# Graph network with masked attention: one q tile of each head turned by VectorE and DMAs instead of TensorE, and one weight set held

## The reference, cut to what matters

```python
h = jnp.maximum(_layernorm(x, axis=-1), 0.0)
q, k, v = (h @ W + b for each), split in 8 heads of 32
scores = einsum('bqhd,bkhd->bhqk', q, k) * 32 ** -0.5
scores = masked by adj            # -inf in layer 2, -1e9 in layer 3
attn = softmax(scores)            # 1024 x 1024 for each head and batch
out = einsum('bhqk,bkhd->bqhd', attn, v) @ Wo + bo
x = x + out                       # layer 2: + out + layernorm(out)
```

## Time and profile before

| | |
|---|---|
| median of 3 runs | 2798.15 us (2797.14 to 2798.94) |
| the profiled execution | 2797.58 us |
| its span | 2795.7 us |
| TensorE busy | 2762.8 us (99%) |
| VectorE busy | 2250.6 us (81%) |
| ScalarE busy | 2062.7 us (74%) |
| GpSimd busy | 1126.7 us (40%) |
| granted TensorE clock | 0.997 of full speed |
| moved by DMA | 251.32 MB |

### The profile page before, as it was taken

One profiled execution on the slowest core, in us unless ns is written; L12 is line 12 of the kernel. 1 busy time (PEld: TensorE's weight loads), 2 busy tenths in 40 slices (PEclk: granted clock), 3 DMA queues, 4 the chain that ended last, 5 costly groups with the idle time before them and its releaser, 6 DMA issues.

```text
span 2795.7 us, 60283 instructions
## 1 busy us (share of the span) xinstructions
PE 2762.8 (99%) x23520; PEld 2219.0 (79%) x23520; DVE 2250.6 (81%) x4144; ACT 2062.7 (74%) x3711; POOL 1126.7 (40%) x1088
## 2 busy tenths in 40 slices
PE   9999999999999999999999999999999999999998
PEld 7888888687778787878787877787778777778776
DVE  6776766888888888888888888888888888888876
ACT  3000001988888889898889888888888888888886
POOL 2222321225556464637373747242424242415131
PEclk9999999999999999999999999999999999999999
DMA  3001002434343434343434363434344343434333
GB/s 132 31 31 61 31 31 61 103 75 111 78 108 90 108 87 104 88 111 83 116 80 111 87 163 94 103 82 110 83 100 99 90 103 87 110 81 114 85 92 84
DMA packets 170601, 251.32 MB, mean 90 GB/s; under 512 B 33328, under 2 KB 135216, under 8 KB 170320
## 3 DMA queue, kind: packets, MB, share of 16 engines
q1 hardware_dynamic: 169120, 243.14, 34.7%
q0 software_dynamic: 1200, 4.33, 0.5%
HBM read 70.65 MB, written 25.69 MB: 34 GB/s over the span
## 4 chain that ended last, share of the span: by engine, by line
PE 70%; POOL 5%; issue 2%; ACT 2%; DVE 2%; DMA 1%; SPq 0%; POOLq 0%; ACTq 0%; DVEq 0%
PE t_ring_ps L885 28%; PE t_ot_ps L913 15%; PE t_s_ps L872 14%; PE t_ring_ps L855 4%; PE t_ring_ps L856 4%; PE t_ring_ps L857 4%; POOL t_xe L1397 2%; ACT t_T L1074 1%; PE t_ring_ps L945 1%; ACT PT L1080 1%; POOL t_oT_lo L1472 1%; POOL t_ot L1461 1%; DVE t_T L1164 1%; DMA t_R_ot<-inverse_row_sums 1%; DMA inverse_row_sums<-t_rT 1%
## 5 line engine op out<-in xcount | busy, mean ns | idle before, releaser
L1164 DVE CUSTOM_DVE_ANT_0 t_T<-t_s_ps,mask 128x1024 f32<-128x1024 f32 x1024 | 1233.4, 1215 | 114.4 <-PE t_s_ps L872 107.7
L1074 ACT ACTIVATE t_T<-t_T,t_low 128x1024 f32<-128x1024 f32 x1024 | 1170.8, 1150 | 23.5 <-DVE t_low L1164 20.2
L885 PEld LDWEIGHTS t_ring_ps<-ident,t_T 128*128 128x128 f32 x8192 | 933.7, 141 | 213.3 <-issue 72.2
L885 PE MATMUL t_ring_ps<-ident,t_T 128*128 128x128 f32 x8192 | 1088.8, 274 | 7.7 <-ACT t_T L1074 2.8
L1080 ACT ACTIVATE PT<-t_ring_ps 128x512 f32<-128x512 f32 x1376 | 757.3, 597 | 230.0 <-PE t_ring_ps L885 220.5
L872 PE MATMUL t_s_ps<-t_k,t_q 128*128 128x512 f32 x2048 | 727.4, 436 | 1.6 <-DVE t_low L1164 1.5
L1249 DVE COPY PT<-t_ring_ps 128x512 f32<-128x512 f32 x672 | 460.9, 690 | 191.0 <-PE t_ring_ps L885 185.0
L913 PE MATMUL t_ot_ps<-PT,shared 128*32 128x256 f32 x8192 | 494.9, 382 | 0.2 <-ACT PT L1080 0.2
L913 PEld LDWEIGHTS t_ot_ps<-PT,shared 128*32 128x32 f32 x8192 | 240.0, 109 | 217.0 <-ACT PT L1080 45.0
L273 ACT ACTIVATE g_yT_hi<-g_ps 128x512 fp32r<-128x512 f32 x64 | 38.3, 599 | 379.3 <-PE g_ps L205 379.3
L872 PEld LDWEIGHTS t_s_ps<-t_k,t_q 128*128 128x128 f32 x2048 | 309.2, 191 | 5.6 <-DVE t_low L1164 5.0
(11 more groups left out here) (186 smaller groups left out, 3743.3 us busy)
## 6 DMA issues: line engine op xcount, KB each, us to landing
t_q<-t_st_hi SPq DMA_DIRECT2D x256, 128.0 KB, 2.3
t_q<-t_st_lo SPq DMA_DIRECT2D x256, 128.0 KB, 2.4
t_k<-t_st_hi SPq DMA_DIRECT2D x256, 128.0 KB, 2.4
t_k<-t_st_lo SPq DMA_DIRECT2D x256, 128.0 KB, 2.4
t_R_ot<-inverse_row_sums SPq DMA_DIRECT2D x256, 64.0 KB, 2.0
t_oT_raw<-t_ot SPq DMA_DIRECT2D x512, 32.0 KB, 1.9
shared<-x_after_graph_layers SPq DMA_DIRECT2D x8, 1024.0 KB, 6.3
t_xe<-x_after_graph_layers SPq DMA_DIRECT2D x32, 256.0 KB, 3.2
```

The costliest lines, as they stand in the source:

```text
L885: last = nc.tensor.transpose(banks[b][:, i * P:(i + 1) * P], T[u % RING][:, kt * P:(kt + 1) * P], ident[:])
L1074: nc.scalar.activation(T[u % RING][:], T[u % RING][:], ACT.Exp, bias=low[:, u % RING:u % RING + 1], scale=-1.0, accum_out=rsum[:, u:u + 1] ...
L1164: nc.vector.tensor_tensor_reduce(out=T[u % RING][:], in0=s_ps[u % 2][:], in1=mask[:, qt, :], scale=1.0, scalar=3.4e38, op0=ALU.add, op1=AL ...
```

## The change

In each head the q tile 0 (units 0, 8, 16, ... of the job, `FLIPS`) is no longer transposed by TensorE and not copied from PSUM. Once its exponential is done, VectorE transposes its 32x32 blocks into `turned_T` (`turn_T`, one instruction of 128x1024). SyncE writes that tile to DRAM (`move_turned`, one DMA of 512 KB in rows of 512 bytes) and, when it is there, reads it back into `PT` in four DMAs of 128 KB, one for each 32 partitions (`place_turned`). `values` of the next head waits for them. In this way the queries of a tile lie in four chunks of 32 in `PT`; tile 1, which shares its matmuls with tile 0, is copied in the same layout (`from_bank`), and the matmuls over the two tiles read 32 columns at a time.

Of the weights one set is held. Layer 3's are split in job 0 through three small tiles `w_new`, saved in DRAM, and loaded over layer 2's: q, k and v columns in job 7, the output's in job 8.

With it other things move: `values` stands ahead of the block of the group's first unit; the copy of the finished head pair (`copy_ot`) stands at the head of ScalarE's group; the row sums' DMA is split in a write and a later read; `regroup` 0 and the loads of `xe` come at other places of SyncE's order; GpSimd's order changes; tables `EARLY`, `MID`, `NEXT`, `BOTH_ON_ACT` (22 units before, 28 now, none of them a q tile 0) and `RAW_ON_DVE` have new numbers. An output block goes from unit 27 to 19.

```diff
-EARLY = [(1, ("norm", 3)), (11, ("out", 0)), (14, ("out", 1)), (27, ("out", 2)), (30, ("out", 3))]
...
+EARLY = [(1, ("norm", 3)), (11, ("out", 0)), (15, ("out", 1)), (19, ("out", 2)), (26, ("out", 3))]
...
+BOTH_ON_ACT = {2, 6, 10, 11, 13, 14, 15, 17, 18, 19, 22, 25, 26, 27, 30, 33, 34, 39, 41, 42, 43, 46, 50, 53, 54, 59, 62, 63}
+RAW_ON_DVE = {20, 34, 37, 49, 52}
+FLIPS = (0,)
...
-                if key[0] == "T" or key[2] in table:
+                if key[2] in table if key[0] == "B" else key[2] % 8 not in FLIPS:
...
-        w_hi = [as_weights(split[0]), sb("w_hi1", [P, DC, 4 * D], F32R)]
-        w_lo = [as_weights(split[1]), sb("w_lo1", [P, DC, 4 * D], F32R)]
+        w_hi, w_lo = as_weights(split[0]), as_weights(split[1])
+        w_new = [sb(f"w_new{i}", [P, 2, DC, D], F32R) for i in range(3)]
...
+        turned_T = [sb(f"turned_T{i}", [P, N]) for i in range(len(FLIPS))]
...
+        def in_chunks(qt):
+
+            return qt in FLIPS or qt ^ 1 in FLIPS
+
         def pt_of(u, half):
 
             qt, keys = u % NT, slice(half * HT, (half + 1) * HT)
-            return PT[:, qt, keys, :] if u // NT % 2 == 0 else PT[:, keys, qt, :]
+            tiles = PT[:, qt, keys, :] if u // NT % 2 == 0 else PT[:, keys, qt, :]
+            return tiles.rearrange("p g (k q) -> p k g q", k=HT) if in_chunks(qt) else tiles
+
+        def from_bank(ps, u):
+
+            return ps[:].rearrange("p (k g q) -> p k g q", k=HT, g=4) if in_chunks(u % NT) else                 ps[:].rearrange("p (k q) -> p k q", k=HT)
...
-            def spread_rows(job, pr, key):
+            def move_turned(job, h, i):
+
+                n = HEADS * job + h
+                sp.wait_ge(T_turned[i], n + 1)
+                if n:
+
+                    sp.wait_ge(turned_in[i], 64 * n)
+                sp.dma_start(turned_rows[i].rearrange("c p f -> p c f"),
+                             turned_T[i][:].rearrange("p (c f) -> p c f", c=NT)).then_inc(turned_out[i], 16)
+
+            def place_turned(job, h, i):
+
+                n, qt = HEADS * job + h, FLIPS[i]
+                sp.wait_ge(turned_out[i], 16 * (n + 1))
+                if n:
+
+                    sp.wait_ge(av_done, NT * (n - 1) + (HT if qt < HT else NT))
+                for j in range(4):
+                    rows = slice(j * HD, (j + 1) * HD)
+                    sp.dma_start(PT[rows, qt, :, :] if h % 2 == 0 else PT[rows, :, qt, :],
+                                 turned_rows[i][2 * j:2 * j + 2].rearrange("h (g k) f -> k (h g) f", g=4)).then_inc(turned_in[i], 16)
...
+            def save_weights(i):
+
+                sp.wait_ge(w_split, i + 1)
+                for part in range(2):
+                    sp.dma_start(w_scratch[part][:, :, i * D:(i + 1) * D],
+                                 w_new[i % len(w_new)][:, part].bitcast(F32)).then_inc(w_saved[i % len(w_new)], 16)
+
+            def load_weights(cols):
+
+                for i in range(len(w_new)):
+                    sp.wait_ge(w_saved[i], 32 * len(range(i, 4, len(w_new))))
+                for part, to in enumerate((w_hi, w_lo)):
+                    sp.dma_start(to[:, :, cols].bitcast(F32), w_scratch[part][:, :, cols]).then_inc(w_late, 16)
...
+                move_head(job, 0)
                 if before is not None:
-                    for p in range(XE):
-                        load_xe(job - 1, before, p)
-                    spread_rows(job - 1, 3, key_of(job, ("norm", 3)))
+                    write_rows(job - 1, 3, key_of(job, ("norm", 3)))
+                place_head(job, 0)
+                if before is not None:
+                    read_rows(job - 1, 3)
                     regroup(job - 1, 3, (0,))
                 load_head(job, 2, UNITS * job + 8, None)
                 if before is not None:
                     regroup(job - 1, 3, (1,))
+                move_head(job, 1)
                 if after is not None:
 
                     sp.wait_ge(v_moved, job + 1)
@@ -795,32 +861,60 @@
                     sp.dma_start(xa[:], x_of(after, job + 1 - B * after).rearrange("(t p) d -> p t d", p=P)).then_inc(xa_in, 16)
                 if before is not None:
                     regroup(job - 1, 3, (2, 3))
+                place_head(job, 1)
                 load_head(job, 3, UNITS * job + 16, None)
-                spread_rows(job, 0, key_of(job, ("norm", 0)))
+                if job == 0:
+                    save_weights(0)
+                    save_weights(1)
+                move_head(job, 2)
+                write_rows(job, 0, key_of(job, ("norm", 0)))
+                place_head(job, 2)
+                read_rows(job, 0)
                 if before is not None:
                     store(job - 1, before, 0, key_of(job, ("out", 0)))
                     after_store(job - 1, 0)
                     load_xe(job - 1, before, 3)
+                if job == 0:
+                    save_weights(2)
+                    save_weights(3)
                 load_head(job, 4, UNITS * job + 24, (job, 1))
+                if layer != after and after is not None:
+                    load_weights(slice(0, 3 * D))
+                move_head(job, 3)
+                place_head(job, 3)
...
+                move_head(job, 7)
                 regroup(job, 2)
+                place_head(job, 7)
...
+                if u % NT in FLIPS:
+                    return
...
+                if kt == 0:
+
+                    for i in range(len(FLIPS)):
+                        pe.wait_ge(turned_in[i], 64 * (NT * job + u // NT))
                 for j in range(HT):
-                    probs = PT[:, 2 * j:2 * j + 2, kt, :] if h % 2 == 0 else PT[:, kt, 2 * j:2 * j + 2, :]
+                    pair = slice(2 * j, 2 * j + 2)
+                    if in_chunks(2 * j):
+                        chunks, cols = slice(kt // HT * HT, (kt // HT + 1) * HT), slice(kt % HT * HD, (kt % HT + 1) * HD)
+                        probs = PT[:, pair, chunks, cols] if h % 2 == 0 else                             PT[:, chunks, pair, cols].rearrange("p g t q -> p t g q")
+                    else:
+                        probs = PT[:, pair, kt, :] if h % 2 == 0 else PT[:, kt, pair, :]
...
                     scores(job, u + 2)
-                    block_of(u)
                     if u >= NT or before is not None:
                         for w in range(u, u + GROUP):
                             values(job, w)
+                    block_of(u)
...
                     exp(job, u + 1)
+                    if u % (2 * NT) == NT - GROUP and (u >= NT or before is not None):
+                        copy_ot(UNITS * job + u + GROUP - NT)
                     exp(job, u + 2)
...
+                was = UNITS * job + u - RING
+                if was >= 0 and was % NT in FLIPS:
+                    dve.wait_ge(T_turned[FLIPS.index(was % NT)], was // NT + 1)
...
+            def turn_T(job, u):
+
+                if u % NT not in FLIPS:
+                    return
+                i, n = FLIPS.index(u % NT), HEADS * job + u // NT
+                dve.wait_ge(p_done, UNITS * job + u + 1)
+                if n:
+
+                    dve.wait_ge(turned_out[i], 16 * n)
+                nc.vector.transpose(turned_T[i][:].rearrange("p (j c q) -> p c j q", j=4, c=NT),
+                                    T[u % RING][:].rearrange("p (c j q) -> p c j q", j=4, c=NT)).then_inc(T_turned[i], 1)
+
...
                     masked(job, u + 2)
                     finish_of(u, ("norm", "out", "v", "qk"))
-                    finish_of(u, ("h",))
                     if u not in BOTH_ON_ACT:
                         copy_pt(job, u)
+                    turn_T(job, u)
                     masked(job, u + 3)
                     if u + 1 not in BOTH_ON_ACT:
                         copy_pt(job, u + 1)
+                    finish_of(u, ("h",))
                     finish_of(u + 1, ("norm", "out", "v", "qk"))
                     finish_of(u + 1, ("h",))
                     finish_of(u + 2, ("h",))
...
+                if before is not None:
+                    scale_ot(job - 1, 3)
                 move_v(job)
                 if before is not None:
-                    scale_ot(job - 1, 3)
                     if before == 1 and job == B + 1:
                         pool.wait_ge(bias_late, 16)
-                    for p in range(XE):
-                        bias_xe(job - 1, before, p)
+                    bias_xe(job - 1, before, 0)
                     turn(job - 1, 0)
+                    bias_xe(job - 1, before, 1)
+                    bias_xe(job - 1, before, 2)
                     turn(job - 1, 1)
...
```

More of the change, by code:

```diff
@@ L518, in bank_plan, with attention_phase @@
     return place
-def attention_phase(nc, a, x_mid, x_mid2, out, mask, shared, ident, PT, split, x_left, row_scratch):
+def attention_phase(nc, a, x_mid, x_mid2, out, mask, shared, ident, PT, split, x_left, row_scratch, turned_rows, w_scratch):
     B, N, D = a["x"].shape
@@ L612, in attention_phase @@
         turned = sem("turned")
```

(35 more changed lines are left out.)

94 lines of the change are left out of this document (51 added, 43 removed).

## The result

| | before | after |
|---|---|---|
| median | 2798.15 us | 2772.78 us of 5 runs (2761.82 to 2778.22) |
| ratio, 95% interval | | 0.9907 (0.9884 to 0.9931) |
| the profiled execution, its span | 2797.58, 2795.7 us | 2772.78, 2771.0 us |
| TensorE's granted clock, mean | 0.997 | 0.990 |

What follows compares the result with a forecast made beforehand. TensorE, 99% busy, was taken as the bound. Savings of 3.1 us in each of eight layer 2 jobs and 4.0 in eight of layer 3, 57 less 5 for weights, took 2797.6 to 2745 us; range 2680 to 2800.

Steps and rivals of the forecast that it cites:

- the lateness of the tile in head 1: SyncE's queue delays head 1's write and reads, so head 2's `values` wait: taken as 1.0 us a job.
- at the longest landings: Head 1's tile comes 2 us late for head 2's `values` at these, by nothing at the short ones.
- the weights: Eight saves of 256 KB and four loads, delaying head 3's tile in job 7: 5 us once, saves included.
- 5.0 us, which is the time of the landing anyway: Head 7: eight of `regroup` stand between the tile's write and its reads, taking no longer than the write's landing.
- 3% on four heads: Heads 0, 3, 4 and 7, set by in-order ScalarE and VectorE handing tiles over: 1.8 us a job added.
- The heads: Each head's length by its latest engine: TensorE in 1, 2, 5, 6, VectorE or ScalarE in others; sum 137.6 us.
- The VectorE transpose: One 128x1024 float32 instruction a head on VectorE: 1.2 us, 9.6 a job, paid by the removed copies.
- the estimate of 2.5 us from the bf16 figure for one block: VectorE transpose as eight 128x128 instructions at the skill's 311 ns; weighed against the 1.2 us taken.
- rival 2: The VectorE transpose costs 2.63 us, the upper bound, making the kernel slower at 2816 us; chance 0.05.
- The chunks of 32 columns in `PT`: Layout for a quarter of the value matmuls and tile 1's copies: no cost; up to 1.86 us a group left to the tail.
- Rival 1: TensorE keeps setting all heads, so the full 117 us of transposes is gained, less 5: 2686 us; chance 0.28.
- Rival 3: The tile comes late in most heads, some 12 us a job, making the kernel slower at 2926 us; chance 0.10.

Runs made afterwards that it cites:

- experiment 2: Changed kernel with only head 1's load of x (1 MB) issued behind the four reads of the turned tile: 2777.62 us, ratio 0.9932 to the kernel before.
- experiment 4: Changed kernel with head 1's write between load_head's q and k parts and its reads ahead of x and regroup 2 and 3: 2732.49 us, ratio 0.9766.
- experiment 3: Changed kernel with only head 1's write moved earlier, between load_head's q and k DMAs, x still ahead of the reads: 2753.13 us, ratio 0.9837.
- experiment 1: Changed kernel without the turned tile's DMAs and the waits for them; VectorE still transposes, contents stale: 2702.55 us, ratio 0.9658.
- experiment 6: Changed kernel without the turned tile's DMAs, the waits for them, and VectorE's transpose: 2699.7 us, ratio 0.9651.
- experiment 5: Changed kernel with FLIPS empty, so all tiles go through TensorE; new tables, orders and weights through DRAM stay: 2793.73 us, ratio 0.9987.
- experiment 8: As experiment 4, with job 7's head 7 tile kept on TensorE, first saves behind head 2's tile, weight loads split behind heads 3 to 5: 2720.52 us, ratio 0.9724.
- experiment 7: As experiment 4, without the save and load of layer 3's weights, so layer 3 computes with layer 2's: 2725.78 us, ratio 0.9747.

## Why the prediction was wrong in size

**The step that failed** is the lateness of the tile in head 1, "I take 1.0 us a job": it cost 3.1. The mechanism was named and is the one in the trace, link by link; its size was not. The pieces, counted from the head-0 start, in job 3 and in brackets as means of jobs 1 to 14: write out 23.5 us forecast, measured 21.6 (22.2); the reads start at 28, measured 26.2 (27.0); end by 34, measured 35.1 (34.0); TensorE asks at 32, measured 31.3 (31.7). The queue was faster than I had it. The landing was not: I took 3.2 us for the last read, the row of a 256 KB load at ordinary times, and it was 6.6 us (5.3), at a DMA share of 1.05. What slows it is mainly the load of x just ahead: with x behind the reads it is 2.9 us in experiment 2 and 2.8 in experiment 4, and with x ahead and the write earlier still 4.5 in experiment 3. My 2 us "at the longest landings" was no upper end, since it used medians of each transfer alone. And from 0 to 2 I chose the middle.

The wait at head 2's `values` came out at 2.5 us a job, the mean of jobs 1 to 14. Against experiment 1, heads 1 and 2 are together 43 us longer in these 14 jobs, 3.1 a job. The other 0.6 us a job is about what TensorE at half clock costs: in six of these jobs `values` alone took 8 us more in all than in the others. I had priced the wait and nothing behind it, although I had named what is queued there.

**The second miss** is job 7, where I had only the weights. I set its head 7 with the other heads, "5.0 us, which is the time of the landing anyway", while the mask load with 8.7 us stood in the earlier trace rows as the bound of another tile's landing, not as traffic of its own: eight such loads go out around the time of that write. That one wait, 8.7 us, made the head 9 us longer. That the masks are its cause is read from the trace, not shown by a run.

**The third** went the other way. I added 3% on four heads, 1.8 us a job in layer 2 and 1.3 in layer 3, 25 us in all, for ScalarE and VectorE handing tiles to each other. The job came out at 137.2 us without it. Experiment 6 shows that VectorE sets neither head 0 nor head 3, and in heads 3 and 4 the chain of experiment 1 is TensorE's alone. ScalarE in heads 7 and 0 was seen rightly: the chain runs over it there, busy for 14.50 of 14.60 us in head 0. What that costs is in the lengths of these heads; there was no more to add.

The sum of it, from experiment 1's span and head lengths:

| | forecast | measured |
|---|---|---|
| nothing late, no adder | 2699 | 2702.5 (experiment 1) |
| adder for two in-order engines | +25 | 0 |
| heads 1 and 2, the late tile | +16 | +43 |
| job 7, heads 3 and 4 (weights) and head 7 (masks) | +5, job 0 with it | +4 and +9 |
| job 0 | in the 5 | +3 |
| head 7 of other jobs, 0 to 0.9 us each, and the rest | 0 | +11 |
| sum | 2745 | 2772.5 |

The lower rows took 49 us more than was forecast, and the adder that wasn't needed hid 25 of them. That the forecast missed by no more than 27 us is in that part luck.

**What was right.** The heads: 14.3, 17.3, 21.1, 15.5, 16.0, 19.6, 19.5, 14.3 forecast, 14.6, 16.7, 21.4, 15.3, 15.9, 19.6, 19.6, 14.1 with nothing late. For heads 0, 3 and 4 the length is partly luck, since VectorE and ScalarE were to set them: with VectorE's transposes gone heads 0 and 3 don't move (experiment 6), and the chain through 3 and 4 is TensorE's. The VectorE transpose, 1.2 taken and 1.231 measured; the estimate of 2.5 us from the bf16 figure for one block was twice too high, and rival 2 is dead. The write's landing in the ordinary case: 3.6 us, under my 4.4. The chunks of 32 columns in `PT`: `values` takes 382 ns a matmul in experiments 1, 5 and 8, with and without the turned tile, and 389 in the change only through the half clock. The weights: 5 us taken, some 7 by the medians of experiment 7. The Trainium skill ("DMA: Bandwidth & Descriptors", Anatomy of one DMA) states its fixed and variable cost for DMAs that GpSimd issues; the estimate of 3.2 us for 512 KB that I worked out from it for SyncE's write is near the median of 3.6. The 6.6 us for 128 KB in the chain shows that such a figure does not hold for a landing in company, and by it head 1 would not have been late.

**The rivals.** Rival 1 was right that TensorE sets heads 1 to 6, and the chip gives 2702.5 when nothing is late. Its 2686 us was too low: it counts 7.3 us a job for the transposes, and experiments 5 and 1 show 6.0, least in heads 0, 2 and 7. Rival 3, the tile late in most heads, holds for head 1 alone and for job 7. The outcome lies between the forecast and it: 3.1 us a job, with 4 as the point of no gain.

## What to carry to other kernels

When a transfer is added to a queue that already carries one issue every 0.6 us, price its landing with everything that is issued in the same ten microseconds, not with the median of its kind; and count behind a wait of TensorE of a few us the time at half clock as well. The order of the queue is then worth more than the bytes: moving the write and the four reads gave back 40 of the 70 us that were lost, and moving the megabyte behind the reads alone gave none, because the next transfer behind it was waited for instead. Before a transfer is moved ahead of another, ask who waits for the one that it pushes back. Where one place is out of line, as job 7 with its masks, look in the trace for what else is issued there, and leave the new work out of that place.
